# A selective state-space layer on one core: one inflow product per unit moved from GpSimd to TensorE, inflows written in place, and three pairs of half-width instructions joined

## What is computed

```python
def _ssm(u, Wdbc, Wdt, bdt, Alog, Dp):
    dbc = jnp.einsum('bse,re->bsr', u, Wdbc)
    dlt, Bm, Cm = jnp.split(dbc, [R, R + N], axis=-1)
    delta = jax.nn.softplus(jnp.einsum('bsr,er->bse', dlt, Wdt) + bdt)
    A = -jnp.exp(Alog)
    dA = jnp.exp(delta[..., None] * A)
    dBu = delta[..., None] * Bm[:, :, None, :] * u[..., None]

    def step(h, xs):
        dA_t, dBu_t, C_t = xs
        h = dA_t * h + dBu_t
        y = jnp.einsum('ben,bn->be', h, C_t)
        return (h, y)
...
    return ys.swapaxes(0, 1) + u * Dp
```

## Time and profile before

| | us |
|---|---|
| median of 3 runs (3417.97 to 3419.03) | 3418.44 |
| profiled execution, its own time | 3421.84 |
| its span, first to last instruction | 3419.9 |
| first scan starts | 284.3 |
| last scan ends | 3368.1 |

### The profile page before, as it was taken

The page is one execution under the profiler, slowest core; times in us unless marked ns, Lnnn a source line. Parts: engine busy times, 40 slices in busy tenths (PEclk is TensorE's granted clock), DMA queues, the critical chain, the costliest instruction groups (busy, mean ns, idle before and its releaser), DMA issues.

```text
span 3419.9 us, 47738 instructions
## 1 busy us (share of the span) xinstructions
PE 2908.9 (85%) x16208; PEld 2093.8 (61%) x16208; DVE 3102.0 (91%) x2079; ACT 2654.8 (78%) x5070; POOL 3127.1 (91%) x1416
## 2 busy tenths in 40 slices
PE   8987888888887888889888888888888888888888
PEld 3554666566666656666666665566666665566665
DVE  2547999999999999999999999999999999999994
ACT  0346899988887888987777889887777899987772
POOL 1336999999999999999999999999999999999996
PEclk9988999999998999999999999999999999999999
DMA  5575344645576344745567334645567444645553
GB/s 216 179 249 199 131 155 153 257 152 183 185 256 233 131 145 149 254 158 171 169 229 241 131 140 165 247 154 169 182 212 242 139 148 159 248 152 162 184 193 120
DMA packets 225131, 628.12 MB, mean 184 GB/s; under 512 B 22300, under 2 KB 68572, under 8 KB 220536
## 3 DMA queue, kind: packets, MB, share of 16 engines
q1 hardware_dynamic: 222440, 606.19, 51.8%
q0 software_dynamic: 2304, 16.78, 1.3%
q10 hardware_dynamic: 144, 2.10, 0.2%
HBM read 544.34 MB, written 80.63 MB: 183 GB/s over the span
## 4 chain that ended last, share of the span: by engine, by line
POOL 33%; issue 23%; PE 22%; DVE 13%; ACT 0%; POOLq 0%; DVEq 0%; ACTq 0%
POOL dbu L1169 18%; POOL hbuf L1174 15%; DVE hbuf L1273 7%; PE y L864 7%; PE mb L835 6%; DVE slot L1273 3%; PE slot L875 3%; PE mb L913 1%; DVE du L1224 1%; PE mb L916 1%; DVE delta L1214 1%; PE mb L958 1%; POOL skip L1180 0%; PE slot L958 0%; PE y L958 0%
## 5 line engine op out<-in xcount | busy, mean ns | idle before, releaser
L1169 POOL TENSOR_TENSOR dbu<-bst,du 128x1024 f32<-128x1024 f32 x640 | 1506.0, 2371 | 64.3 <-DVE du L1224 54.8
L1174 POOL TENSOR_TENSOR hbuf<-hbuf,cres 128x1024 f32<-128x1024 f32 x640 | 1507.1, 2372 | 37.2 <-DVE hbuf L1273 36.0
L864 PE MATMUL y<-ident,hbuf 128*128 128x128 f32 x8192 | 1121.7, 287 | 251.5 <-POOL hbuf L1174 248.4
L864 PEld LDWEIGHTS y<-ident,hbuf 128*128 128x128 f32 x8192 | 993.1, 148 | 444.6 <-POOL hbuf L1174 339.2
L1085 ACT ACTIVATE abuf<-dut,bt 128x128 f32<-128x128 f32 x3072 | 971.3, 388 | 0.0
L1273 DVE TENSOR_TENSOR_SCAN hbuf<-dec,slot 128x1024 f32<-128x1024 f32 x384 | 874.3, 2277 | 40.3 <-PE slot L875 22.4
L1273 DVE TENSOR_TENSOR_SCAN slot<-slot,dbu 128x1024 f32<-128x1024 f32 x384 | 875.5, 2280 | 9.4 <-ACT slot L1133 4.7
L1133 ACT ACTIVATE slot<-delta,par 128x1024 f32<-128x1024 f32 x640 | 710.5, 1110 | 194.4 <-DVE hbuf L1278 179.9
L875 PE MATMUL slot<-ident,abuf 128*128 128x128 f32 x3072 | 427.6, 285 | 182.4 <-ACT abuf L1085 172.6
L1273 DVE TENSOR_TENSOR_SCAN hbuf<-slot,dbu 128x1024 f32<-128x1024 f32 x256 | 580.3, 2267 | 1.2 <-ACT slot L1133 1.2
L1133 ACT ACTIVATE dec<-delta,par 128x1024 f32<-128x1024 f32 x384 | 438.5, 1142 | 161.9 <-DVE hbuf L1273 161.8
(11 more groups left out here) (149 smaller groups left out, 2111.7 us busy)
## 6 DMA issues: line engine op xcount, KB each, us to landing
bst<-bc_s SPq DMA_DIRECT2D x640, 512.0 KB, 4.3
cres<-bc_s SPq DMA_DIRECT2D x128, 512.0 KB, 8.2
wzs<-wz_s SPq DMA_DIRECT2D x64, 256.0 KB
yf_s<-yrd SPq DMA_DIRECT2D x32, 512.0 KB, 5.4
ybuf<-yf_s SPq DMA_DIRECT2D x32, 512.0 KB, 6.0
yg_s<-ybuf SPq DMA_DIRECT2D x31, 512.0 KB, 3.0
si_s<-silu SPq DMA_DIRECT2D x28, 512.0 KB, 6.1
silu<-si_s SPq DMA_DIRECT2D x28, 512.0 KB, 4.5
```

The source lines that it names most:

```text
L864: last = nc.tensor.matmul(y[:, j * P:(j + 1) * P], hbuf[:, q % HR, j * P:(j + 1) * P], ident[:], start=False, stop=(q % N == N - 1), is_tr ...
L1169: nc.gpsimd.tensor_tensor(dbu[:, i % DR, :], bst[:, i % BR, :], du[:, k % 2, :], ALU.mult).then_inc(pool_b, 1)
L1174: nc.gpsimd.tensor_tensor(hbuf[:, q % HR, :], hbuf[:, q % HR, :], cres[:, q % N, :], ALU.mult).then_inc(pool_prod, 1)
```

## The change

Three edits to `ssm_kernel` (and one tile that moves in `setup_kernel`).

1. Chunk 1 of every unit becomes kind **E**. Its inflow comes from PE: eight plain fp32 128x128 matmuls (`spread_inflow`), `dut` block times `diag`, a diagonal matrix of B's column for state 1, into `slot[1]`. It waits until that slot's last reader, chunk 15 of the unit before (its product on DVE), is done, and stands first at PE's step 1. Its decay goes to `dec`. `diag` is made on ACT by eight 128x128 instructions once per direction and sequence (8 times in all): once ahead of the first unit, then at step 14 of the last unit of each group of 8. POOL keeps the product of chunk 1 with C, and has 9 inflows in a unit, no longer 10.
2. Inflows are written in place over the B row. `bst` has 5 tiles, `dbu` is gone, and a B row is loaded over tile i only after scan i has read it; SP waits for that scan two steps later. `inflow_step` still looks three pooled chunks ahead.
3. `finish_delta`, `gate_y` and the Abs at the start of softplus run once over 1024 elements. Their semaphores count one per unit.

`rows` of the setup moves into a part of `xn2` to make room.

```diff
-KINDS = "VPVVAVAPAVAPAPAV"
+KINDS = "VEVVAVAPAVAPAPAV"
+SPREAD = KINDS.index("E")
-BR = 3
+BR = 5
-POOLED = [q for q in range(NU * N) if kind(q) != "A"]
-TURNED = [q for q in range(NU * N) if kind(q) == "A"]
+POOLED = [q for q in range(NU * N) if kind(q) in "VP"]
+TURNED = [q for q in range(NU * N) if kind(q) in "AE"]
...
-                    if kind(q) != "A" and before("VP", q) + BR < len(POOLED):
-                        i = before("VP", q)
-                        sp.wait_ge(pool_b, i + 1)
-                        load_b(i + BR)
+                    if q >= 2 and kind(q - 2) in "VP" and before("VP", q - 2) + BR < len(POOLED):
+                        sp.wait_ge(scanned, q - 1)
+                        load_b(before("VP", q - 2) + BR)
...
+            def spread_inflow(q):
+                pe.wait_ge(dut_ready, 2 * (q // N) + 2)
+                pe.wait_ge(diag_ready, q // SEQ + 1)
+                if q >= 2:
+                    wait_scanned_out(pe, q - 2)
+                for j in range(ET):
+                    last = nc.tensor.matmul(slot[q % 2][:, j * P:(j + 1) * P], dut[:, j * P:(j + 1) * P], diag[:, j, :],
+                                            start=True, stop=True)
+                last.then_inc(turned, 1)
...
                     if kind(q) == "A":
                         turn_inflow(q)
+                    elif kind(q) == "E":
+                        spread_inflow(q)
...
-                for h in range(2):
-                    act.wait_ge(dps_mm, 2 * k + h + 1)
-                    nc.scalar.activation(soft[:, half(h)], mb[h][:], ACT.Abs).then_inc(soft_step, 1)
+                act.wait_ge(dps_mm, 2 * k + 2)
+                nc.scalar.activation(soft[:], mbw[:], ACT.Abs).then_inc(soft_step, 1)
...
+            def make_diagonal(g):
+                act.wait_ge(bt_ready, g + 1)
+                if g > 0:
+                    act.wait_ge(turned, before("AE", (g * ET - 1) * N + SPREAD + 1))
+                for j in range(ET):
+                    last = nc.scalar.activation(diag[:, j, :], ident[:], ACT.Copy, scale=bt[:, g % 2, j, SPREAD:SPREAD + 1])
+                last.then_inc(diag_ready, 1)
...
+            make_diagonal(0)
...
+                        if c == 14 and new_b:
+                            make_diagonal((k + 1) // ET)
...
-                if i >= DR:
-                    pool.wait_ge(scanned, POOLED[i - DR] + 1)
-                nc.gpsimd.tensor_tensor(dbu[:, i % DR, :], bst[:, i % BR, :], du[:, k % 2, :], ALU.mult).then_inc(pool_b, 1)
+                nc.gpsimd.tensor_tensor(bst[:, i % BR, :], bst[:, i % BR, :], du[:, k % 2, :], ALU.mult).then_inc(pool_b, 1)
...
-                for h in range(2):
-                    nc.vector.scalar_tensor_tensor(out=delta[:, k % 2, half(h)], in0=mb[h][:], scalar=0.0,
-                                                   in1=soft[:, half(h)], op0=ALU.max, op1=ALU.add).then_inc(delta_ready, 1)
+                nc.vector.scalar_tensor_tensor(out=delta[:, k % 2, :], in0=mbw[:], scalar=0.0, in1=soft[:],
+                                               op0=ALU.max, op1=ALU.add).then_inc(delta_ready, 1)
...
-                for h in range(2):
-                    bank = mb[h][:] if k < NU - 1 else slot[0][:, half(h)]
-                    dve.wait_ge(ytr_mm, 2 * pair(k) + h + 1)
-                    nc.vector.tensor_tensor(ybuf[:, half(h)], bank, silu[:, half(h)], ALU.mult).then_inc(gated, 1)
+                bank = mbw if k < NU - 1 else slot[0]
+                dve.wait_ge(ytr_mm, 2 * pair(k) + 2)
+                nc.vector.tensor_tensor(ybuf[:], bank[:], silu[:], ALU.mult).then_inc(gated, 1)
...
-                    if kind(q) == "A":
-                        dve.wait_ge(turned, before("A", q + 1))
+                    if kind(q) in "AE":
+                        dve.wait_ge(turned, before("AE", q + 1))
                         decays, inflows = dec, slot[q % 2]
...
-                        decays, inflows = slot[q % 2], dbu[:, before("VP", q) % DR, :]
+                        decays, inflows = slot[q % 2], bst[:, before("VP", q) % BR, :]
```

More of the change, by code:

```diff
@@ L50, in setup_kernel @@
         bfb = sb("bfb", [P, D])
-        rows = sb("rows", [B, 7, D])
         ct = sb("ct", [P, KE * B])
@@ L523, in ssm_kernel @@
         slot = [ctx.enter_context(nc.psum_tensor(f"slot{i}", [P, S], fp32)) for i in range(2)]
-        mb = [ctx.enter_context(nc.psum_tensor(f"mb{i}", [P, TC], fp32)) for i in range(2)]
+        mbw = ctx.enter_context(nc.psum_tensor("mb", [P, S], fp32))
+        mb = [mbw[:, 0:TC], mbw[:, TC:S]]
         b_in, unit_in, xn_in, dl_in, ones_ready = (t[n] for n in ("b_in", "unit_in", "xn_in", "dl_in", "ones_ready"))
@@ L707, in store_dbc @@
                                  dbc[R:RD, d, :]).then_inc(dbc_out, 16)
-            for i in range(BR):
-                load_c(0, i)
+            for n in range(3):
+                load_c(0, n)
             for k in range(NU):
@@ L934, in project @@
                 for e in es:
-                    last = nc.tensor.matmul(bank[:], yp_tile(i)[:, e, :], wf[:, e, :], start=(e == 0), stop=(e == ET - 1))
+                    last = nc.tensor.matmul(bank, yp_tile(i)[:, e, :], wf[:, e, :], start=(e == 0), stop=(e == ET - 1))
                 if ET - 1 in es:
@@ L1059, in sigmoid_half @@
                 act.wait_ge(mx_mm, i + 1)
-                nc.scalar.activation(soft[:, half(h)], mb[h][:], ACT.Relu,
+                nc.scalar.activation(soft[:, half(h)], mb[h], ACT.Relu,
                                      bias=par[:, 0, k % ET, PBX:PBX + 1]).then_inc(sig_step, 1)
@@ L1097, in copy_dut @@
                 if k > 0:
+                    act.wait_ge(turned, before("AE", (k - 1) * N + SPREAD + 1))
+                if k > 0:
                     act.wait_ge(scaled, len(SCALE_STEPS) * k - 1 + h)
-                nc.scalar.activation(dut[:, half(h)], mb[h][:], ACT.Copy).then_inc(dut_ready, 1)
+                nc.scalar.activation(dut[:, half(h)], mb[h], ACT.Copy).then_inc(dut_ready, 1)
             def evict_dbc(j, d):
```

53 lines of the change are left out of this document (28 added, 25 removed).

## The result

The change makes the kernel slightly faster: the median is **3410.02 us** (7 runs, 3406.64 to 3411.62) against 3418.44 for the kernel before in the same session (7 runs, 3414.35 to 3423.10). The ratio is 0.9971, 95% interval 0.9961 to 0.9981, so 0.29% faster; the two medians alone give 0.9975, inside the interval. The forecast was 3405, range 3370 to 3436. The profiled execution of the changed kernel has a span of 3408.4 us, against 3419.9.

A forecast was written before the change was run, and what follows sets the result against it. POOL, with DVE just behind, was taken as the bound, then DVE and PE's order. Terms -13, -16.5, +9, +5+2 and 0 made -13 from 3421.84: 3409, then 3405 as runs' median is 3.4 lower; range 3370 to 3436.

The forecast's parts named there:

- 28 M units: Units 2 to 8, 18 to 24, 34 to 40, 50 to 56: 0.41 us less DVE wait, 0.05 from joined halves each; -13.
- 22 units with `finish_result`: Per unit 2.3 us of waits for POOL gone, 0.1 from joined halves, 1.65 added at scan 1; together -16.5 us.
- units 10 to 15: Six units at POOL's pitch and DVE's busy time at once: +1.65-0.1 us each, together +9.
- group ends' diagonals: At the end of 7 groups, scalings ahead of decay 15 and a `copy_dut` exceed slack by 0.5 to 0.9 us: +5.
- up to the first scan: Eight diagonal scalings ahead of unit 0 delay decay 0 and scan 0 by about 2.1 us; +2 in the sum.
- the wait at scan 1: After P or D units the spread stands behind PE's whole projection, so DVE waits 1.65 us, bounds 1.3 and 2.3.
- The lower bound, 1.3: Smallest wait allowed at scan 1 after P or D units, taken without the semaphore steps between engines.
- Rival 3: M units gain nothing because scan 1 or scan 14 picks up what was saved, margins being thin; 3418, chance 0.17.
- The spread's price: Chunk 1's eight plain fp32 products on PE, 16 records: 1.74 us, and 0.16 to the end of the last.
- The estimate by that page: With transposes 4 times faster for fp32, PE's spread would take 3.5 us and not 1.74.
- The rest, 0: Units 0, 1, 16 and the tail, where DMA and PE set the pace, were given no change.
- Rival 2: Spread on PE before scan 1 longer than its rows; gain gone at about 0.4 us, extreme 3495; chance 0.20.

The follow-up runs named there:

- the fourth run: Changed kernel with POOL issuing the inflows of chunks 13 and 15 one pooled chunk earlier; 3392.58 us, 0.9919 of the kernel before.

## Why the prediction was right, and where it was not

The direction, the size (3405 against 3410) and the order of the parts came out. Term by term, between first scans of units, in the two profiled executions:

| term | predicted | measured |
|---|---|---|
| 28 M units | -13 | -2.4 |
| 22 units with `finish_result` | -16.5 | -13.8 |
| units 10 to 15 | +9 | +10.6 |
| group ends' diagonals | +5 | within the rows above |
| up to the first scan | +2 | +6.2 |
| units 0, 1, 9, 16, 25, 41, 57, 63 | 0 | -12 |
| sum | -13 | -11.5 |

- **Units with `finish_result`: right.** The gating's waits went, scan 1's came; 48.78 us a unit, and 48.8 predicted. Two errors cancel in it: the wait at scan 1 is 0.3 us longer than put, and without it a unit lasts 46.84 us and not the 47.2 of the sum. Putting chunk 1 back on POOL brought the old waits back.
- **Units 10 to 15: right in mechanism**, 48.18 and predicted 48.2, again with a longer wait and a shorter rest (46.23 us and not 46.57). That the change makes some units longer was the main point of the argument.
- **The wait at scan 1: 1.95 us, predicted 1.65**, inside the bounds. (The lower bound, 1.3, does not follow from the terms: without the steps between engines they give 13.42-11.93 = 1.5.) Over the program these waits are 58.3 us, against the 46 that the prediction named. Product 12 started at 1710.41 (1705.75 + 2 x 2.33), 0.3 us after scan 12 ended, since POOL was still at products 10 and 11. I had taken POOL as relieved enough. The earlier inflows of the fourth run then showed that PE alone needs as long. The cause of the wait, PE's order, is shown by moving the spread: 38 us, of which about 34 lie at these boundaries.
- **M units: the step that failed.** The prediction said that POOL "now waits for scan 7" and then "has five operations". It waits for scan 6 and has six, 14.0 us from 1356.91, which ends where it did before. The trace of the kernel before had this already. POOL in unit 22 there:

```profile
1347.03 4.69 POOL L1174 TENSOR_TENSOR hbuf<-hbuf,cres 128x1024 f32<-128x1024 f32 x2 [0.55 <-DVE hbuf L1273]
```

Product 6 waits for scan 6, and six operations from 1347.03 end at 1361.0, where PE's wait of the earlier trace rows ends: product 10 was held by scan 6, not by how much POOL has to do. The saved 2.33 us became POOL's idle 2.07 us at 1354.8, before work that could not start earlier, and nothing of it reached product 10. The run with inflows 13 and 15 earlier filled that gap, and the wait went. Rival 3's place was right, but its cause was another: not a margin elsewhere, but saved time that fell ahead of a wait.
- **The waits at scan 8 of the M units** did go, 9.9 us, and the wait at scan 14 took their place. They went with a slow clock: between scans 4 and 8 the mean granted clock was 0.71 or 0.72 in 9 of those 13 units and 0.86 in the other 4. In unit 19 PE, after 1.99 us idle for POOL, took 3.37 us for four records of 512 columns ahead of chunk 8's turn, with a granted clock of 0.50 from 1204 to 1206 us; in unit 22, with 1.00 at that place, they took 1.90. With the change 27 of the 28 M units have 0.85 or 1.00 there. That relieving POOL acted in part through PE's clock is a reading that no run isolates.
- **The spread's price: right.** 1.95 us for 16 records by the row, 1.74+0.16 predicted; doubling cost 1.81 us a place. In this trace eight plain products take 1.95 us and eight transposes 1.04. That is a factor of 1.9. The Trainium skill, page "TensorE: Matmul & The Clock Gate", section Terms, has the transpose mode 4 times faster for fp32. The estimate by that page was 3.5 us, and the trace does not agree.
- **Diagonals.** 2.34 us from start to start ahead of unit 0 (287.04 to 289.38), as predicted; 0.96 us at the group ends after M units and 1.35 in the others, predicted 0.5 to 0.9. Over the steady units DVE's waits for ACT rose from 2.2 to 8.0 us, so 5.8 where the sum had 5.
- **"The rest, 0": wrong.** Unit 16 became 3.5 us shorter and unit 63 6.2 (56.49 to 50.30); I had left them out as paced by DMA and PE. Unit 1 became 1.8 shorter. With chunk 1 back on POOL 2.9, 4.4 and 0.9 us of this stay, and with the halves apart these units are nearly as short (47.67, 46.90 and 50.09), so most of it belongs to the tiles in place and their loads or to the joined Abs, not to the moved chunk; which of them, no run says. The start was 4 us later than predicted, but kernels with the same loads and diagonals ahead of unit 0 start anywhere from 286.3 to 290.5 us, so one profiled execution of each cannot price it. These errors and that of the M units nearly cancel: that the total came so close is in part luck. POOL waited for a row of B only once, 1.6 us, as the sum had it.
- **Rival 2** had the right prices: with 1.81 us more a place the loss was 100 us, about 45 of it at the boundaries after M units, where scan 1 then waits 1.49 us at most of them, so that the slack was the 0.3 us that the text gives. Its break-even of 0.4 us was not tested.
